# Feed-forward output: residual copied to the output in memory and results added to it by GpSimd's accumulating transfers, instead of an identity product on TensorE

## The reference

```python
def fp4_linear(x, w):
    return einsum('bsk,nk->bsn', fp4_quant_dequant(x), fp4_quant_dequant(w))

gate = fp4_linear(z, w_gate)        # z = layernorm(x), 256 -> 704
y = fp4_linear(z, w_up)             # 256 -> 704
h = silu(gate) * y
out = x + fp4_linear(h, w_down)     # 704 -> 256, and the residual x
```

## Time and profile before

| | us |
|---|---|
| median of 3 runs (3495.25 to 3504.69) | 3501.41 |
| profiled execution | 3504.35 |
| its span | 3502.5 |
| PE busy in it | 3190.3 (91%) |
| DVE busy | 2476.6 (71%) |
| ACT busy | 1443.6 (41%) |
| GpSimd busy | 893.5 (26%) |

### The profile page before, as it was taken

One profiled execution on the slowest core, in us unless ns is written; L12 is line 12 of the kernel. 1 busy time (PEld: TensorE's weight loads), 2 busy tenths in 40 slices (PEclk: granted clock), 3 DMA queues, 4 the chain that ended last, 5 costly groups with the idle time before them and its releaser, 6 DMA issues.

```text
span 3502.5 us, 145112 instructions
## 1 busy us (share of the span) xinstructions
PE 3190.3 (91%) x64386; PEld 2381.6 (68%) x64386; DVE 2476.6 (71%) x5588; ACT 1443.6 (41%) x3274; POOL 893.5 (26%) x1045
## 2 busy tenths in 40 slices
PE   7875899999599999999999999999999999978999
PEld 4654899999366666666666666666666666656666
DVE  6775111120488888888888888888888888886997
ACT  1221222221245455545544555455445554543443
POOL 2235122221123222322232223222332232221000
PEclk9886999999799999999999999999999999999999
DMA  2115666667100000000000000000000000010100
GB/s 67 49 50 186 196 185 185 188 183 252 29 6 11 8 10 8 11 8 10 8 11 8 10 8 11 8 10 8 11 8 10 8 11 8 8 48 10 32 26 17
DMA packets 97900, 168.31 MB, mean 48 GB/s; under 512 B 15241, under 2 KB 71689, under 8 KB 97025
## 3 DMA queue, kind: packets, MB, share of 16 engines
q1 hardware_dynamic: 76688, 136.01, 11.8%
q0 software_dynamic: 19440, 21.97, 4.4%
q10 hardware_dynamic: 1152, 1.06, 0.1%
HBM read 118.80 MB, written 38.09 MB: 45 GB/s over the span
## 4 chain that ended last, share of the span: by engine, by line
PE 35%; DVE 32%; issue 6%; ACT 1%; POOL 0%; DVEq 0%; ACTq 0%; POOLq 0%
DVE da_eGn L1289 8%; DVE da_z L1288 8%; PE da_unit L1750 5%; PE da_C L1920 4%; PE da_unit L1950 4%; PE da_unit L1836 3%; PE da_A L1891 3%; PE da_B L1907 2%; PE da_A L1868 2%; DVE da_M L1312 2%; PE da_B L1898 2%; PE da_B L1880 2%; PE da_B L1881 1%; PE da_unit L1816 1%; DVE da_eGn L1292 1%
## 5 line engine op out<-in xcount | busy, mean ns | idle before, releaser
L1132 POOL TENSOR_TENSOR da_M<-da_M,da_decay 128x512 f32<-128x512 f32 x256 | 261.1, 1046 | 795.7 <-DVE da_TT L1294 439.7
L1546 ACT COPY da_Ub<-da_U 32x256 f32<-32x256 f32 x992 | 399.3, 403 | 16.5
L1289 DVE TENSOR_TENSOR da_eGn<-da_eGn,da_z 128x30 f32<-128x30 f32 (+14 forms) x960 | 328.3, 342 | 33.0
L1288 DVE TENSOR_TENSOR da_z<-da_eGn 128x30 f32<-128x30 f32 (+14 forms) x960 | 329.6, 343 | 27.7
L1750 PE MATMUL da_unit<-early_buffer,da_xnT 128*128 128x512 f32 x512 | 284.9, 642 | 9.7 <-DVE da_sp L1230 6.4
L1920 PE MATMUL da_C<-da_Ub,da_Km 128*64 128x256 f32 x1984 | 290.6, 411 | 1.5 <-issue 0.9
L1537 ACT COPY da_U<-da_A 128x256 f32<-128x256 f32 x256 | 95.3, 372 | 424.7 <-PE da_A L1891 424.6
L840 PEld LDWEIGHTS le_ps_qkv<-le_scr,le_up 128*128 128x128 f32 x2272 | 265.7, 193 | 4.8 <-ACT le_scr L670 1.8
L840 PE MATMUL le_ps_qkv<-le_scr,le_up 128*128 128x128 f32 x2272 | 267.7, 276 | 1.2 <-ACT le_scr L670 1.2
L1891 PEld LDWEIGHTS da_A<-da_W,da_TT 32*32 32x32 f32 x8192 | 127.5, 105 | 187.6 <-DVE da_W L1307 66.8
L1758 PE MATMUL da_unit<-da_xnT,early_buffer 128*128 128x128 f32 x2048 | 242.2, 277 | 9.9 <-ACT da_eGn L1529 9.9
(11 more groups left out here) (315 smaller groups left out, 7000.0 us busy)
## 6 DMA issues: line engine op xcount, KB each, us to landing
le_up<-in_upT SPq DMA_DIRECT2D x71, 1024.0 KB, 5.0
le_scr<-moe_slots SPq DMA_DIRECT2D x71, 129.0 KB, 4.2
le_down<-in_downT SPq DMA_DIRECT2D x8, 1024.0 KB, 12.1
early_buffer<-in_x SPq DMA_DIRECT2D x16, 256.0 KB, 4.2
moe_acc<-le_y SPq DMA_DIRECT2D x32, 128.0 KB, 2.3
da_x<-moe_acc SPq DMA_DIRECT2D x128, 32.0 KB, 1.8
stream<-da_xz SPq DMA_DIRECT2D x128, 32.0 KB, 1.6
stream<-da_y POOLq DMA_DIRECT2D x128, 32.0 KB, 2.8
```

The source lines that it names most:

```text
L1132: ins = nc.gpsimd.tensor_tensor(st_, st_, decay[:, par, rec, 2 * g:2 * g + 2].rearrange("p a b -> p (a b)").unsqueeze(2).to_broadcast([P, ...
L1288: c.link(tt(t, Xm[:, s + 1:C, s:s + 1].to_broadcast([P, below, s]), Xm[:, s:s + 1, 0:s].to_broadcast([P, below, s]), ALU.mult))
L1289: c.link(tt(Xm[:, s + 1:C, 0:s], Xm[:, s + 1:C, 0:s], t, ALU.add))
L1546: ins = nc.scalar.copy(Ub[rows_of(b), :, :, b, :], U[rows_of(b), rec])
```

## The change

The residual no longer goes through TensorE. For each trip SP copies the 512 KB of residual rows in memory from `x_out` to `out` (`fill_trip`), and each tile's result is added to them there by a GpSimd transfer with `accum_op=ALU.add` (`add_out`), which waits for the copy (`filled`) and for the result (`y_ready`). The identity matmul is gone, and the first matmul with `downT` begins the sum. SP's loop no longer stores tiles: it loads and copies trip by trip, with the same wait on `y_ready` for a load and one more on `zs_ready`. The first two copies wait for the weights' load (`w_loaded`), and the load of trip 2 now stands behind them.

```diff
@@ semaphores
+        filled = [m.sem(f"filled{i}") for i in range(XB)]
@@ block.sync
+            def fill_trip(t):
+                sp_.dma_start(trip_rows(out, t), trip_rows(x_out, t)).then_inc(filled[t % XB], 16)
+
             sp_.wait_ge(v_psum, 2 * NCH)
             load_trip(0)
             load_trip(1)
             sp_.dma_start(packed, consts["ff_weights"]).then_inc(w_loaded, 16)
-            for t in range(TRIPS):
-                if t + 2 < TRIPS:
-                    if t > 0:
-                        sp_.wait_ge(y_ready, t * UN)
-                    load_trip(t + 2)
-                for u in range(UN):
-                    sp_.wait_ge(y_ready, t * UN + u + 1)
-                    sp_.dma_start(tile_rows(out, t, u), ys[:, u, :]).then_inc(stored[u], 16)
+            sp_.wait_ge(w_loaded, 16)
+            fill_trip(0)
+            fill_trip(1)
+            for t in range(2, TRIPS):
+                if t > 2:
+                    sp_.wait_ge(zs_ready, (t - 2) * UN)
+                    sp_.wait_ge(y_ready, (t - 2) * UN)
+                load_trip(t)
+                fill_trip(t)
             for u in range(UN):
                 sp_.wait_ge(stored[u], 16 * TRIPS)
@@ block.gpsimd
             put_out(LAST)
-            for t in range(1, TRIPS):
-                scales(t)
+
+            def add_out(n):
+                t, u = divmod(n, UN)
+                pool.wait_ge(filled[t % XB], 16 * (t // XB + 1))
+                pool.wait_ge(y_ready, n + 1)
+                pool.dma_start(tile_rows(out, t, u), ys[:, u, :], accum_op=ALU.add).then_inc(stored[u], 16)
+
+            for n in range(NT + 2):
+                if n % UN == 0 and n // UN + 1 < TRIPS:
+                    scales(n // UN + 1)
+                if n >= 2:
+                    add_out(n - 2)
@@ block.tensor, down(n)
-                mm(ps_y[:, 0:D], ident[:], xs[:, (n // UN) % XB, n % UN, :], start=True, stop=False)
                 for k in range(IC):
                     width = min(P, I - k * P)
-                    ins = mm(ps_y[:, 0:D], hqT[0:width, n % 2, k, :], downT[0:width, k, :], start=False, stop=(k == IC - 1))
+                    ins = mm(ps_y[:, 0:D], hqT[0:width, n % 2, k, :], downT[0:width, k, :], start=(k == 0), stop=(k == IC - 1))
```

More of the change, by code:

```diff
@@ L1018, in delta_and_feed_forward @@
         ps_g, ps_u = [A[:, 0:512], A[:, 512:1024]], [Cp[:], un[:, 2]]
-        xs_loaded = [m.sem(f"xs_loaded{i}") for i in range(XB)]; w_loaded = m.sem("w_loaded"); fvar_ready = m.sem("fvar_ready"); nb_ready = m.sem("nb_ready"); zs_ready = m.sem("zs_ready"); made = m.sem("made")
+        xs_loaded = [m.sem(f"xs_loaded{i}") for i in range(XB)]; filled = [m.sem(f"filled{i}") for i in range(XB)]; w_loaded = m.sem("w_loaded"); fvar_ready = m.sem("fvar_ready"); nb_ready = m.sem("nb_ready"); zs_ready = m.sem("zs_ready"); made = m.sem("made")
         zexpo_ready = m.sem("zexpo_ready"); zabove_ready = m.sem("zabove_ready"); qz_ready = m.sem("qz_ready"); zT_psum = m.sem("zT_psum"); zT_ready = m.sem("zT_ready")
```

## The result

| | before | after |
|---|---|---|
| median | 3501.41 us | 3513.8 us |
| lowest to highest (7 runs each) | 3495.25 to 3508.67 | 3508.25 to 3518.26 |
| span of the profiled execution | 3502.5 us | 3512.0 us |
| trip 0's `KT` (DVE) to the end of the span | 318.89 us | 326.48 us |

The ratio of the times is 1.0031, with a 95% interval of 1.0018 to 1.0045: the change makes the kernel some 11 us slower (6 to 16). On another chip, in twelve runs, the same kernel came out at 1.0018 (1.0005 to 1.0030), so a loss of about 0.05 to 0.45% is what is known. The forecast was 3504.3 us in a range of 3495.8 to 3513.0. The median lies 0.8 us above that range; by the ratio, 3501.41 x 1.0031 = 3512.3 us, it lies just inside. Either way the forecast of +2.9 us missed most of the loss.

A forecast was written before the change was run, and what follows sets the result against it. The prediction took DVE and one ACT handover per trip as the bound, TensorE only in trip 1 and the end. Terms -0.4 - 2.6 + 2.1 = -0.9, plus 3.8 for two clock falls, gave +2.9: 3504.3 us, range 3495.8 to 3513.0.

The forecast's parts named there:

- falls of the clock: TensorE's clock in the feed-forward drops to half behind longer gaps, costing 1.9 us each in the middle trips.
- The way out: After ACT's last copy: GpSimd's later start and slower landing than SP's store add 2.1 us, bounds 1.3 to 3.9.
- Start: Trip 1, TensorE's clock at half speed: 0.43 us of DVE's 3.61 us wait goes; -0.4 us in the sum.
- End: Last tiles, after some 3457 us, where TensorE sets the pace: 1.7 us plus 0.86 us come through, together 2.6 us.
- Trips 2 to 6 bring nothing: Middle trips: DVE and one ACT handover set the pace, so TensorE only waits longer for `KT`; 0 us.
- The gaps: TensorE's wait before the transposes of `KT` grows from 1.13 to 2.9 us per trip, 1.9 us after a fall.
- two falls: Likeliest case: the clock falls twice in the five middle trips, 2 x 1.9 = 3.8 us; chance 0.37.
- GpSimd's 32 issues: Feed-forward: issues of up to 1.55 us each on a nearly idle GpSimd cost 0 us.
- Copies: Eight 512 KB memory copies on SP's queue, 4 to 8 us each, issued two trips (75 us) ahead, cost 0 us.
- Slower, by DVE held up: Rival: GpSimd issues delay DVE's fast-mode instructions, up to 1.0 us in 28 tiles; +28 us, 3529 us; chance 0.08.
- the tail over 4 us: Rival: the program's end costs over 4 us; chance 0.05, shared with copies late.
- the late copies: Rival: a copy takes over 65 us and adds wait each trip, 3515 us or more; shares chance 0.05.

The follow-up runs named there:

- the memset: Kernel before, plus one GpSimd memset of one column that waits for the last result; 1.0020 (1.0007 to 1.0032) of the kernel before.
- additions by DVE: Kernel before, but in the last six tiles no identity product, and DVE adds the residual in place of ACT's copy; 1.0002 (0.9989 to 1.0014).
- the first profile: Profiled execution of the changed kernel in its first runs, against the kernel before; span 3512.0 us, ratio of those runs 1.0031.
- the last trip by SP: Changed kernel, but the last trip's four tiles keep identity product and SP store, without that trip's copy; 1.0003 (0.9989 to 1.0016) of the kernel before.
- the run with 28 issues and TensorE's work unchanged: Changed kernel with last trip stored by SP and identity product put back as unread work in the other 28 tiles; 1.0000 (0.9987 to 1.0013) of before.

## Where the prediction was right and where it missed, step by step

By the ratio the time came out inside the stated range, but not by the forecast's mechanism. The range's upper end is there for falls of the clock, a slower landing and one fall more; the loss came from the way out, whose own bounds were passed. That they meet is luck. (The upper end is also 0.2 us more than its terms: 3509.1 + 1.8 + 1.9 = 3512.8.)

- **The way out: forecast 2.1 us (bounds 1.3 to 3.9), measured 7.4 us.** This is the term that failed. Its parts were nearly right: GpSimd's record starts 0.5 us after ACT's copy instead of 0.29 us, landing 3.1 us instead of 3.6. With these, a path that ends at the landing would have cost 1.9 us. But I let the path end there, as it had for SP's stores. With the last work on GpSimd the path goes through GpSimd's closing, 7.9 us, which outlasts the landing by more than 5 us. The row was in the trace of before, 11.3 us long, under work that lasted longer. The prediction moved an engine's last instruction from 72 us before the end to the very end and asked only what that instruction costs, not what stands behind it.
- **Start, -0.4 us: no run shows it.** Where the clock stayed in trip 1, the trip took 37.45 us with the product (the runs with the memset and with additions by DVE) and without it (three others): nothing to gain. Where it fell, DVE's wait there went from 3.61 us to 1.68, 1.93 and 2.00 us, since its low stretch was 3.4 us instead of 6.8; that gave 1.9 us back in the first profile, and it is the clock's doing.
- **End, -2.6 us: 1.7 of it shown, the rest not.** In the two profiles without any product and without a fall before, DVE's fourth wait of trip 7 ended 33.39 us after `KT` instead of 35.11: 1.72 us, as reckoned. Behind it the clock fell in both, so the last 0.86 us never came through at full clock. With the last trip by SP, where only part of the products is gone, `KT` to the last copy took 51.45 us, 1.3 us less, without a fall. In the first profile 0.9 us came through, because the clock fell behind the gap of trip 7 too.
- **Trips 2 to 6 bring nothing: right.** 37.42 to 37.47 us per trip wherever the clock didn't fall, with and without the product.
- **The gaps: forecast 2.9 us, and 1.9 us after a fall; measured 2.91 and 1.92 us.** What the prediction concluded from the second figure, that falls come at most in every other trip, was wrong: the clock fell in trips 5, 6 and 7 in a row, two of them behind gaps of 1.9 us. Nor is a fall worth a fixed 1.9 us, a price that was read from a low stretch of 6.8 us. DVE's extra wait was 1.97 us in trip 5, whose low stretch was as long, but 0.39 us in trip 3 (wait of 1.69 us) and 0.7 us in trip 6, low for 3.4 us each. Together 3.1 us, near the 3.8 us forecast for two falls because a wrong count (three, not two) and a wrong price offset each other. What I hadn't seen at all is that falls differ from one execution to the next: several have none in trips 1 to 6 and one in the last tiles instead.
- **GpSimd's 32 issues: 0, right.** DVE's L1374, which was L1360, takes 529 ns in the mean; before it was 527 ns (526 in the median both times), and the run with 28 issues and TensorE's work unchanged is as long as the kernel before within 0.4 us. GpSimd's record of an issue is 0.86 us long beside a busy DVE as well as at the very end, where DVE is done. The Trainium skill, page "SBUF — State Buffer", section "SBUF: two separate sides", says that the two engines lock a pair of ports against each other. No row here shows either of them held up by it, and none contradicts it, since the rows don't show when within its 0.86 us an issue needs the ports.
- **Copies: 0, right.** 5.5 us in a lead of 75 us.
- **The rivals.** "Slower, by DVE held up" named the right side with the wrong mechanism; "the tail over 4 us" shared a chance of 0.05 with the late copies, with no mechanism or price of its own, and was what happened.

## What to carry to other kernels

Before the last work of a program is moved to another engine, look up how long that engine's closing took in the trace and under what it was hidden: here GpSimd's closing ended 5.4 to 10.5 us after its last instruction, be it a transfer of 128 KB or a memset of 0.1 us, and the program waits for it unless other work lasts longer. Time freed on an engine that isn't the pace becomes a gap at its next wait; on TensorE such a gap can cost the clock, and one length of gap goes either way from one execution to the next, so a single profile decides nothing about it. Where earlier stages vary by more than the change is worth, count from a mark at the start of the changed stage.

## What the runs showed that I hadn't expected

- GpSimd's closing DRAIN ends 10.5 us after a memset or a small tensor instruction, 7.6 to 7.9 us after the last of many accumulating transfers, and 5.4 us after a single plain one.
- An accumulating transfer of 128 KB (128 rows of 1 KB, issued by GpSimd) lands in 3.1 us, only 0.3 us more than one of 32 KB.
- TensorE's clock fell at every gap of 2.89 to 3.50 us in three profiles and at none of such gaps in three others, one of them of the same kernel. It fell at half of the gaps of 1.91 to 1.94 us, and in the last tiles at gaps of 2.00 and 2.44 us; none of the gaps of 0.90 to 1.20 us in trips 2 to 7 cost it.
